# A four-layer forward pass on one NeuronCore: second attention and expert layer put into one block, with the order of the expert layer's jobs turned round

## The reference

```python
# third layer: cross attention, 16 heads of 64, 64 keys and one null key; ln_scale, ln_bias
x = x + xattn(layernorm(x), ctx_2048, Wq, Wkv, null_kv, Wout)

# fourth layer: a shared MLP and 2 of 8 experts for every row, on h = layernorm(x)
normed = h * rsqrt(mean(h ** 2) + 1e-8) * norm_weight
shared = relu(normed @ sw1 + sb1) @ sw2 + sb2                       # 128 -> 512 -> 128
scores, idx = top_k(sigmoid(normed @ router_w.T), 2)
w = scores / (sum(scores) + 1e-6)
routed = sum over the two: w * (relu(normed @ ew1[e] + eb1[e]) @ ew2[e] + eb2[e])
x = x + shared + routed
```

## Time and profile before

| what | value |
|---|---|
| median of three runs | 1444.42 us (1444.32 to 1447.08) |
| span of the profiled execution | 1468.5 us |
| PE busy | 1250.4 us (85%) |
| DVE busy | 1054.3 us (72%) |
| ACT busy | 899.3 us (61%) |
| POOL busy | 653.5 us (44%) |

### The profile page before, as it was taken

The page is one execution under the profiler, slowest core; times in us unless marked ns, Lnnn a source line. Parts: engine busy times, 40 slices in busy tenths (PEclk is TensorE's granted clock), DMA queues, the critical chain, the costliest instruction groups (busy, mean ns, idle before and its releaser), DMA issues. The chain is left out here.

```text
span 1468.5 us, 35946 instructions
## 1 busy us (share of the span) xinstructions
PE 1250.4 (85%) x13401; PEld 1041.2 (71%) x13401; DVE 1054.3 (72%) x2080; ACT 899.3 (61%) x1699; POOL 653.5 (44%) x677
## 2 busy tenths in 40 slices
PE   4999998399999999997599999999997268999880
PEld 3777777278777877786489888888886256787660
DVE  5888888566877687675256678989887369676563
ACT  3888887566565666654355655666654248787660
POOL 2222222145655555564332345556755327165561
PEclk9999999689999999999699999999999669999995
DMA  4222221332213221321210000000000123146646
GB/s 143 93 94 93 94 93 64 116 94 80 73 39 92 80 73 37 94 80 44 86 38 17 10 17 9 17 15 18 24 13 17 44 58 89 48 151 217 203 139 182
DMA packets 88373, 109.64 MB, mean 75 GB/s; under 512 B 13322, under 2 KB 55050, under 8 KB 88202
## 3 DMA queue, kind: packets, MB, share of 16 engines
q1 hardware_dynamic: 83210, 97.05, 21.3%
q0 software_dynamic: 4992, 10.30, 2.1%
HBM read 61.70 MB, written 29.82 MB: 62 GB/s over the span
## 5 line engine op out<-in xcount | busy, mean ns | idle before, releaser
L830 POOL TENSOR_TENSOR b_h_lo<-b_h,b_h_hi 128x512 fp32r<-128x512 f32 x168 | 216.3, 1292 | 179.7 <-ACT b_h_hi L854 179.2
L849 ACT ACTIVATE b_zg<-b_zg 128x512 f32<-128x512 f32 x168 | 97.6, 581 | 82.0 <-PE b_zg L894 81.8
L854 ACT ACTIVATE b_h_hi<-b_h 128x512 fp32r<-128x512 f32 x168 | 105.2, 626 | 65.7 <-DVE b_h L1059 65.6
L1059 DVE TENSOR_TENSOR b_h<-b_zg,b_uw 128x512 f32<-128x512 f32 x168 | 116.2, 692 | 32.1 <-ACT b_zg L849 26.8
L2173 POOL DMA_INDIRECT planes_dram<-d_y_out,d_back x92 | 94.5, 1028 | 93.6 <-DVE d_y_out L2484 68.8
L1052 DVE TENSOR_TENSOR b_uw<-b_zu,b_gw 128x512 f32<-128x512 f32 x128 | 88.2, 689 | 57.7 <-PE b_zu L894 50.9
L2453 DVE TENSOR_TENSOR d_h_lo<-d_h,d_h_hi 128x512 fp32r<-128x512 f32 x124 | 85.1, 689 | 44.6 <-ACT d_h_hi L2214 26.8
L312 POOL TENSOR_TENSOR a_qx<-a_qT,headmask 128x256 f32<-128x256 f32 x64 | 37.9, 612 | 150.3 <-ACT a_qT L347 150.3
L519 DVE TENSOR_REDUCE a_top<-a_score_ps 128x8 f32<-128x1024 f32 x64 | 78.1, 1220 | 18.6 <-PE a_score_ps L410 18.6
L1293 POOL TENSOR_TENSOR c_prob<-c_prob,c_recip 128x512 f32<-128x512 f32 x64 | 65.5, 1044 | 50.9 <-DVE c_recip L1709 50.9
L1716 DVE TENSOR_TENSOR c_oT_lo<-c_oy,c_oT_hi 128x512 fp32r<-128x512 f32 x64 | 43.7, 683 | 58.1 <-ACT c_oT_hi L1421 57.5
(11 more groups left out here) (393 smaller groups left out, 4172.3 us busy)
## 6 DMA issues: line engine op xcount, KB each, us to landing
rows_dram<-a_blank SPq DMA_DIRECT2D x32, 520.0 KB, 3.3
b_gw<-gates_dram SPq DMA_DIRECT2D x64, 256.0 KB, 3.9
d_up_slot<-d_up_tab SPq DMA_DIRECT2D x15, 512.0 KB
d_down_slot<-d_down_tab SPq DMA_DIRECT2D x15, 512.0 KB
d_xg<-rows_dram SPq DMA_DIRECT2D x23, 260.0 KB
b_gm<-gates_dram SPq DMA_DIRECT2D x32, 160.0 KB, 3.8
c_craw<-in_c_ctxT_dram SPq DMA_DIRECT2D x16, 256.0 KB, 3.1
d_pay<-planes_dram SPq DMA_DIRECT2D x12, 256.0 KB, 4.3
```

The costliest lines, as they stand in the source:

```text
L830: pool.tensor_tensor(h_lo[:, m % HS, :], h[:, m % HF, :], h_hi[:, m % HS, :].bitcast(F32), ALU.subtract).then_inc(lo_done.sem, 1)
L849: act.activation(zg_ps[:, n % ZG, :], zg_ps[:, n % ZG, :], ACT.Silu).then_inc(sg_done.sem, 1)
L854: act.activation(h_hi[:, m % HS, :], h[:, m % HF, :], ACT.Copy).then_inc(hi_done.sem, 1)
L1059: dve.tensor_tensor(h[:, n % HF, :], zg_ps[:, n % ZG, :], uw[:, n % 2, :], ALU.mult).then_inc(h_done.sem, 1)
```

## The change

`second_half` takes the place of the last two calls. Both stages now stand in one block, with one PSUM tensor (`cd_arena`) and SBUF rooms at fixed offsets, those of the second stage over tensors of the attention that are done. Every engine function is a generator that yields after each step. `in_turn` runs 39 steps (ACT: 38) of the attention, then one step of each in turn for 16 steps, then the rest of the attention and the rest of the second stage:

```diff
+def in_turn(order, first, second):
+    stages = (first, second)
+    for which, steps in order:
+        for _ in range(steps):
+            next(stages[which], None)
...
+        alone = 39
+        order = [(0, 1), (1, 1)] * 16 + [(0, 2), (1, 500)]
...
+        @block.gpsimd
+        def _(pool):
+            in_turn([(0, alone)] + order, first.gpsimd(pool), second.gpsimd(pool))
```

```diff
-ROUTED = 5
...
-    ticks = range(-6, UNITS + 8)
+    ticks = range(-6, UNITS + 18)
...
     def group_at(n, after):
         g, odd = divmod(n - after - 10, GROUP)
-        return g if odd == 0 and 0 <= g < ROUTED else None
+        return g if odd == 0 and 0 <= g < GROUPS else None
...
             for j, (lo, hi) in enumerate(((0, 3), (3, 6), (6, 2 * GROUP))):
                 g = group_at(n, 9 + j)
-                if g is not None and g + 1 < ROUTED:
+                if g is not None:
                     scatter(g, lo, hi)
```

The 18 weight pieces are the first 18 steps of the second stage on ACT, DVE and POOL, and no longer lie beside its jobs:

```diff
+        for i in range(PREP):          # POOL; the same loop stands on ACT and DVE
+            weights.rest(pool, i, i + 1, True)
+            yield
```

The jobs are then the 23 tiles first and the 8 shared MLPs last. The first tile is loaded once the scatters of the last two groups have landed:

```diff
+    JOBS = TILES + GROUPS
...
+            t = k + 1 if k < 0 else k + 2
+            if 0 <= t < TILES:
+                if t == 0:
+                    for g in range(GROUPS - 2, GROUPS):
+                        wait_rows(sp, g)
...
+                sp.dma_start(xg[:, t % 2, :, :], block_rows.rearrange("(u p) f -> p u f", p=P)
+                             ).then_inc(xg_in[t % 2], 16)
```

The planes get SBUF of their own for all groups (`summands`), so all 16 loads are issued when the last tile's scatter has landed, while the shared jobs run. POOL adds the two planes of a group, and DVE adds the sum to x at a step given by `join_step`, two groups per job from job step 27 on:

```diff
+        for g in range(GROUPS):
+            for n in range(2):
+                sp.dma_start(plane(g, n), planes[first:first + COLS, :].rearrange("(u p) f -> p u f", p=P)
+                             ).then_inc(fetched[g], 16)
+        for g in range(GROUPS):
+            sp.wait_ge(summed.sem, summed.at(g + 1))
+            sp.wait_ge(out_done.sem, out_done.at(TILES + g + 1))
+            sp.dma_start(out[g * COLS:(g + 1) * COLS, :].rearrange("(u p) f -> p u f", p=P),
...
+        for g in range(GROUPS):        # POOL
+            pool.wait_ge(fetched[g], 32)
+            pool.tensor_tensor(plane(g, 0), plane(g, 0), plane(g, 1), ALU.add).then_inc(joined.sem, 1)
...
+    def join_step(g):
+        return divmod(CH * (TILES + 4) + 1 + 2 * g, CH)
```

More of the change, by code:

```diff
@@ L20 @@
 from contextlib import ExitStack, contextmanager
+from collections import namedtuple
 from itertools import product
@@ new lines, in sorted_experts @@
+    up_in, down_in = ([sem(f"{n}_in{s}") for s in range(WS)] for n in ("up", "down"))
+    stored, summed = sem("stored"), tally("summed")
+    fetched = [sem(f"fetched{g}") for g in range(GROUPS)]
+    joined = tally("joined")
+    added = [sem(f"added{s}") for s in range(2)]
+    jobs = []
+    for e in [*range(1, E + 1), 0]:
+        for m, (shared, name) in enumerate(((up_shared, "d_w"), (down_shared, "d_wd"))):
+            row = tab[:, e - 1, m, :] if e else shared[:, :]
+            jobs += pieces(row[:, 0:half], row[:, half:W], a[name][:, e * half:(e + 1) * half])
@@ new lines, in sorted_experts, with parts, block_of, bias @@
+    weights = SplitWeights(nc, ctx, tag + "sw", jobs, 3, sw_raw)
+    PREP = len(jobs)
+    def parts(shared, m, slots, k):
+        if k >= TILES:
+            return shared[:, :]
+        return tab[:, k, m, :] if k < E else slots[:, (k - E) % WS, :]
+    def block_of(row, lo, c):
+        return row[:, lo * half + c * P:lo * half + (c + 1) * P]
+    def bias(k, c):
+        if k >= TILES:
+            return b_shared[:, c:c + 1]
+        return b_tab[:, k, c:c + 1] if k < E else b_slot[:, (k - E) % (WS + 1), c:c + 1]
@@ new lines, in sorted_experts, with second_half @@
+    return Programs(sync, gpsimd, scalar, tensor, vector)
+KB = 1024
+def second_half(nc, earlier, x, stats, ident, a, rows, planes, out, route):
+    with stage(nc, earlier) as ctx:
+        base = nc.sbuf_base
+        room = Room(nc, base, nc.sbuf_usable_end - base)
+        arena = ctx.enter_context(nc.psum_tensor("cd_arena", [P, 8, 512], F32))
+        first, marks, wait_rows, scattered = attention1(nc, ctx, earlier, room, arena, x, stats, ident, a, route, rows)
+        finished = [s for s in ctx.taken if s not in scattered]
+        earlier.held.close()
+        at = base
+        rooms = {}
+        for name, size in (("projections", 24 * KB), ("inputs", 28 * KB), ("heads", 32 * KB), ("outputs", 69 * KB),
+                           ("last", 24 * KB)):
+            rooms[name] = Room(nc, at, size)
+            at += size
+        rooms["spare"] = room
+        second = sorted_experts(nc, ctx, rooms, arena, x, ident, a, rows, planes, out, route, marks, wait_rows, finished)
+        alone = 39
+        order = [(0, 1), (1, 1)] * 16 + [(0, 2), (1, 500)]
@@ L2144, in _ @@
-            for g in range(GROUPS):
-                sp.wait_ge(summed.sem, summed.at(2 * g + 2))
-                if g + PAY < GROUPS:
-                    fetch(g + PAY)
-                sp.dma_start(out[g * COLS:(g + 1) * COLS, :].rearrange("(u p) f -> p u f", p=P),
-                             x[:, g * GROUP:(g + 1) * GROUP, :]).then_inc(stored, 16)
-            sp.wait_ge(stored, 16 * GROUPS)
+            in_turn([(0, alone)] + order, first.sync(sp), second.sync(sp))
         @block.gpsimd
@@ L2234, in _ @@
[L2234 removed]
+            in_turn([(0, alone - 1)] + order, first.scalar(act), second.scalar(act))
         @block.tensor
         def _(pe):
[L2238 to L2245 removed]
@@ L2498, in _ @@
-            ticks(step)
-            for g in range(GROUPS):
-                tiles = x[:, g * GROUP:(g + 1) * GROUP, :]
-                dve.wait_ge(fetched[g % PAY], 32 * (g // PAY + 1))
-                for n in range(2):
-                    dve.tensor_tensor(tiles, tiles, pay[g % PAY][:, n, :, 0:C], ALU.add).then_inc(summed.sem, 1)
-                    if n == 0:
-                        dve.wait_ge(summed.sem, summed.at(2 * g + 1))
+            in_turn([(0, alone)] + order, first.vector(dve), second.vector(dve))
@@ L2508, in program @@
+    earlier.sems = [s for s in earlier.sems if s not in finished]
 def program(nc, a, rows, gates, planes, out):
```

2268 lines of the change are left out of this document (1057 added, 1211 removed).

## The result

The kernel after takes 1470.9 us (median of four runs, 1470.7 to 1473.6) against 1445.6 for the kernel before (1444.3 to 1447.1) in the same job, on one chip: a ratio of 1.0175 with a 95% interval of 1.0156 to 1.0193, or 25.3 us slower. The forecast was 14.3 slower, 1458.7. The measured time lies in its wide range (up to 1474), near the end, and 3 us outside the narrower one (1449 to 1468) that it gave for its own account.

The account below looks back on a forecast made before the run. PE bounds the tiles; POOL's routing string delays the first tile. 1250.4 + 3 + 161.5 + 55.0 + 4.3 + 8.6 = 1482.8 against 1468.5, 14.3 slower: 1458.7 on the median, range 1440 to 1474, own range 1449 to 1468.

Parts of the forecast that it names:

- first tile's start, after against before: Behind the attention and routing: first tile's up product at 1250.4, 9.0 us earlier than the 1259.4 before.
- tile phase: The 23 tiles: same work and holes, 161.5 us, plus 3 for the clock.
- shared phase: Eight shared jobs behind the tiles: 55.0 us, from a PE floor of 51.2 (8 × 6.40) plus DVE and POOL terms.
- last up product to the end: Kernel's end: plane loads and sums hidden under shared jobs; 8.6 instead of 43.2 us follow PE's last product.
- Group 5's four multiplies: In the attention, ticks 30 to 33: group 5's multiplies fall where POOL waits for DVE, so cost nothing.
- the walk: POOL's routing string behind the attention: from 1150.8, 70.3 us work plus 20.5 waits, last scatter ending at 1241.6.
- DVE's own load: Shared jobs at the end: DVE needs 7.7 us in two jobs where all coincide, 2.6 too much.
- POOL's sums: Shared jobs at the end: POOL's plane sums can hold DVE up, 0 to 10.2 us, taken as 1.2.
- rival C: Shared jobs: POOL's plane sums hold DVE each time (10.2 instead of 1.2), or planes land late; 1467.7; chance 0.13.
- Rival A: Routing tail: POOL runs densely, only the 4.7 `pay` wait stays; first tile 1234.6, median 1442.9; chance 0.18.
- Rival B: Tile phase: its 14.3 us of holes above 23 × 6.40 go, so no change, median 1444.4; chance 0.07.
- The clock: At the start of the tiles: time lost at the lower clock level, 0 to 12 us, taken as 3.

Follow-up runs that it names:

- the second profile of the kernel before: The kernel before, no edit, timed and profiled again: 1446.1 us, ratio 0.9994 to itself, profiled span 1444.5.
- 54.3 in the second profile: The kernel after, unchanged, timed and profiled again on another chip: 1472.4 us, ratio 1.0164 to the kernel before, span 1467.3.
- thin sums: The kernel after with POOL's eight sums of two planes done over 16 of 512 columns: 1467.4 us, ratio 1.0125 to the kernel before.
- the experiment that takes out the payload wait: The kernel after with a second buffer for payload rows (groups 5 and 7) and a second destination list: 1458.9 us, ratio 1.008 to the kernel before.

## Why the prediction was right and where it failed

The direction and its cause are right: the gain at the end is real, and the shared jobs, put behind the tiles, cost more than it. The size is 11 us short, and that the time still lies in the stated range is owed to the width of that range.

By the timed runs, with the second profile of the kernel before as the base (its span, 1444.5, fits its times; both spans are about 2 below the time), the terms are:

| term | predicted | measured |
|---|---|---|
| first tile's start, after against before | -9.0 | 0.0 (1249.9 and 1249.9) |
| tile phase | +3 | +1.2 (149.3 against 148.1) |
| shared phase | +55.0 | +55.9 |
| last up product to the end | -34.6 (47.5 to 12.9) | -33.0 (46.5 to 13.45) |
| sum | +14.3 | +24.0 |

**The step that failed** is "Group 5's four multiplies stand in ticks 30 to 33, where POOL waits for DVE; nothing." With their reductions they cost the attention 8.5 us at its end, and the string behind it starts that much later. With these multiplications and reductions thinned the attention's end is back (36.6 for two pairs, 36.3 before), and the first tile comes 5.7 us earlier, of the 9.0 by which this term is off. The other 3.3 aren't traced to one edit. The waits of the walk were 3.0 us longer than taken and its work 1.3; it began 3.0 us earlier (1147.8 for 1150.8) and its tail, from the last scatter to the first product, was 7.1 for 8.8. So its end came out right, by errors that cancel.

**Why the error didn't show in the first profile.** I took "9.0 earlier than before" from 1259.4, and 161.5 for the tiles. Both came from an execution 24 us longer than the timed ones, 13.4 of it in the tiles, 7.8 in the attention behind its first copy of y, 2.3 ahead of that. The absolute start, 1250.4, was right for the kernel after by luck: the late attention of that execution stood in for a delay that group 5 really causes. On a clean base group 6 is summed at 1140.5, not 1150.8, and the same walk would have given 1240.1 for the first tile and 14.6 for the whole. In the kernel after POOL begins it 7.3 later than that: the pauses alone did not spoil the sum, the uncosted work did. In the waits of the first profile's tile phase DVE stands idle with nothing that the profile could name:

```profile
DVE d_h_lo L2453 <- issue: 13.5, 11, 4.6
```

What made it pause isn't settled. In the tiles of the other profiles shown here such pauses did not come back.

**The end**: confirmed. The plane loads are hidden, the last store is all that is left, 13.4 from the last up product as said ("some 13").

**The shared phase**: 55.9 for 55.0 (54.3 in the second profile), right in sum and wrong in its parts. With thin sums it is 49.9 (1406.94 to 1456.80), below the floor of 51.2, because the last three turns back come 5.9, 4.9 and 3.7 apart with no further job beside them. So DVE's own load, taken at 2.6, shows no cost, and POOL's sums, taken at 1.2, cost 4.4, or 6.0 with the fall of the clock. The rule of rival C does act; in price C stays below its 10.2.

**Rival A** (a dense POOL) fell as told: the last row scatter ended at 1242.9, far behind 1224. But the experiment that takes out the payload wait brought 12.0 (13.8 in the string itself) and not the 4.7 that the walk gives for that buffer, since the same wait stood, unseen, in front of the compare and of split 5.

**Rival B** (the holes go) happened in the profile and was worth nothing in time, as the holes were not in the timed runs of the kernel before.

**The clock**: 3 taken at the start of the tiles; by the windows the tiles run at 0.99 in the kernel after and in the second profile of the one before, and the phases differ by 1.2.

## What to carry to other kernels

Compare the profiled span with the timed median before using a profile as a base: 24 us too much is not an offset but a set of pauses at places of their own, and a sum that subtracts stage by stage inherits them. A wait that one buffer causes can stand in several places of a string, under the names of other engines; price it by all of them (12.0 here, where its own line showed 6.0). And when work moves out from under a long stream, look at both ends: here half of the shared work at the front and half at the end, with the payload buffer and the splits moved, turned a loss of 25 us into a gain of 6 (0.44%, interval 0.31 to 0.58%).

## What the runs showed of the hardware

An indirect DMA costs POOL 0.96 and 0.30 to the next under an empty PE; under a full one, in the tiles, the median of 92 is 0.97 and the longest 1.33. POOL's sum of two 128x512 operands lengthens DVE operations that read two SBUF operands (0.68 to as much as 1.78 us) or norm from SBUF (1.11 to as much as 3.15 for four), while DVE's relu out of PSUM stays at 0.74 and its sum of a PSUM and an SBUF operand at 0.68 (at 1433.65). And not expected at all: two profiles of one kernel can agree within 1.2 us of span (1468.5 and 1467.3) or differ by 24 (1468.5 and 1444.5).
